# Expert outputs added to rows of the output in memory, a narrower table, 28 rooms, and first weights copied by VectorE alone

## The reference

```python
h = _layernorm(x, axis=-1) * (1 + ca) + sa
x = x + ga * _L0_attn_ref(h, ...)        # 16 heads of 8 features, softmax over 256 tokens
h = _layernorm(x, axis=-1) * (1 + cb) + sb
x = x + gb * _L0_ffn_ref(h, ...)         # 14 experts, each token goes to one
```

## Time and profile before

| | us |
|---|---|
| median of 3 runs | 610.19 (608.88 to 610.45) |
| span of the profiled execution | 609.06 |
| attention loop's last exponential ends | 491.7 |
| first turn that needs a late load (visit 12) | 522.73 |
| last turn (visit 76) | 594.32 |
| last contraction starts | 598.06 |
| last store starts | 601.75 |

### The profile page before, as it was taken

One profiled execution on the slowest core, in us unless ns is written; L12 is line 12 of the kernel. 1 busy time (PEld: TensorE's weight loads), 2 busy tenths in 40 slices (PEclk: granted clock), 3 DMA queues, 4 the chain that ended last, 5 costly groups with the idle time before them and its releaser, 6 DMA issues.

```text
span 609.1 us, 12013 instructions
## 1 busy us (share of the span) xinstructions
PE 471.5 (77%) x2535; PEld 266.9 (44%) x2537; DVE 555.4 (91%) x1419; ACT 545.2 (90%) x2323; POOL 484.3 (80%) x642
## 2 busy tenths in 40 slices
PE   5456887877887777788788788778776688989993
PEld 2113433333343333333334343334333366889992
DVE  5898999999999999999999999999999978788884
ACT  2599999999999999999999999999999963767882
POOL 4566777998999989899998989989898765677763
PEclk9555556566556756655655655675555565999997
DMA  6365544544455555555555555665555215888750
GB/s 194 104 189 157 138 140 125 139 138 140 141 149 148 148 152 140 163 142 167 146 156 149 148 154 148 173 172 145 160 149 152 93 65 143 269 281 255 223 180 27
DMA packets 77072, 94.42 MB, mean 155 GB/s; under 512 B 12806, under 2 KB 60710, under 8 KB 76998
## 3 DMA queue, kind: packets, MB, share of 16 engines
q1 hardware_dynamic: 68842, 75.69, 45.0%
q0 software_dynamic: 6144, 16.82, 7.4%
q10 hardware_dynamic: 2015, 1.15, 0.7%
HBM read 58.41 MB, written 35.20 MB: 154 GB/s over the span
## 4 chain that ended last, share of the span: by engine, by line
ACT 48%; POOL 17%; DVE 12%; PE 11%; issue 8%; DMA 2%; ACTq 1%; POOLq 0%; DVEq 0%; SPq 0%
ACT scores L927 47%; DVE neg_max L1395 4%; PE scores L1223 4%; PE scores L1232 4%; POOL table L838 3%; POOL xhat L787 2%; POOL rstd L770 2%; POOL rest L577 2%; POOL parts L580 2%; POOL h_scaled L810 1%; DVE y_biased_s L1966 1%; DMA table<-rows,place_i 1%; PE scores L1213 1%; POOL xhat L779 1%; POOL att L799 1%
## 5 line engine op out<-in xcount | busy, mean ns | idle before, releaser
L927 ACT ACTIVATE scores<-scores,neg_max 128x256 f32<-128x256 f32 x1024 | 468.5, 827 | 10.5 <-DVE neg_max L1395 10.4
L927 ACT ACTIVATION_READ_ACCUMULATOR scores<-scores,neg_max 128x1 f32 x1024 | 436.2, 588 | 0.0
L1395 DVE TENSOR_REDUCE neg_max<-scores 128x4 f32<-128x1024 f32 x256 | 309.2, 1211 | 7.5 <-PE scores L1073 7.0
L1073 PE MATMUL scores<-k_stack,q_stack 64*128 64x256 bf16 x1024 | 148.5, 389 | 79.3 <-ACT scores L927 67.7
L1073 PEld LDWEIGHTS scores<-k_stack,q_stack 64*128 64x128 bf16 x1024 | 34.0, 106 | 164.3 <-ACT scores L927 120.6
L838 POOL DMA_INDIRECT table<-rows,place_i x64 | 66.0, 1031 | 20.4 <-issue 17.0
L787 POOL TENSOR_SCALAR xhat<-rows,mv,rstd 128x128 f32<-128x128 f32 x60 | 47.6, 796 | 7.1 <-POOL rstd L770 7.1
L893 POOL DMA_INDIRECT out_dram<-x_s x40 | 39.4, 986 | 17.4 <-DVE x_s L1977 9.2
L1232 PE MATMUL scores<-w_s,hid 128*128 x308 | 49.8, 286 | 2.2 <-DVE y_biased_s L1966 1.1
L1101 PE MATMUL side_a<-w_gated,opt_t 128*128 128x128 f32 x128 | 49.7, 491 | 0.0
L779 POOL TENSOR_SCALAR xhat<-x_s,mv,rstd 128x128 f32<-128x128 f32 x62 | 49.1, 801 | 0.4 <-POOL rstd L770 0.4
(11 more groups left out here) (231 smaller groups left out, 876.0 us busy)
## 6 DMA issues: line engine op xcount, KB each, us to landing
q_stack<-parts_dram SPq DMA_DIRECT2D x192, 64.0 KB, 2.9
x_s<-table SPq DMA_DIRECT2D x62, 192.5 KB
parts_dram<-parts SPq DMA_DIRECT2D x31, 384.0 KB, 3.0
k_stack<-parts_dram SPq DMA_DIRECT2D x186, 64.0 KB, 2.2
mod_b<-mod_rows SPq DMA_DIRECT2D x32, 256.0 KB, 4.4
x_s<-in_x_dram SPq DMA_DIRECT2D x13, 256.0 KB, 4.8
table<-pad_tile SPq DMA_DIRECT2D x15, 192.5 KB
more_rooms<-table SPq DMA_DIRECT2D x15, 192.5 KB
```

Of the source, the lines that this page charges most:

```text
L927: last = act.activation(buf[:, k * L:k * L + L], buf[:, k * L:k * L + L], ACT.Exp, bias=neg_max[:, p, n:n + 1], accum_out=exp_sum[:, p, n: ...
L1073: last = pe.matmul(scores[:, c, at:at + L], q_stack[p][r, g + j, t * P:t * P + P], k_stack[p][r, g + j, :], start=True, stop=True)
L1395: dve.tensor_reduce(to, scores[:, (PAIRS * b.n + i) % RING, :].rearrange("p (e j m) -> p e j m", e=2, j=2), AX_X, ALU.max, negate=True).th ...
```

## The change

- **Adding stores.** `store` and `store_packed` get `compute_op=ALU.add`: the indirect DMA adds the rows to what lies in the output. `out_y` goes, and `gate_y` writes in place into the room; it is written one step later, where `out_y` stood.
- **x2 is stored by itself.** `residual` writes x2 into a ring of two tiles. SP stores it to the output as it is, in token order, one plain DMA per batch (`store_x2`), ahead of `store_parts`. `residual` waits for the store of two batches before; GpSimd waits for all of these stores before its first adding ones. The wait for `scattered` moves from `residual` to where h2 is written (`modulate2`, `shift_h2`).
- **Narrow rows.** ROW is 257 words: h2, GW and ID. Scatters, pads and loads shrink by a third.
- **28 rooms.** All lie over x; `more_rooms` goes.
- **First weights.** VectorE copies them for all visits. `by_act`, `fetched` and `fetch_shared` go, with ScalarE's loads of expert numbers.

```diff
-H2, X2, GW, ID = 0, D, 2 * D, 3 * D
-ROW = 3 * D + 1
+H2, GW, ID = 0, D, 2 * D
+ROW = 2 * D + 1
...
-MORE = 5
-ROOMS = SLOTS + MORE
+ROOMS = 28
...
+            def store_x2(b):
+
+                r = b.slot(RING_X2)
+                sp.wait_ge(x2_ready, b.done())
+                sp.dma_start(out_tiles[:, LT * b.n:LT * b.n + LT, :], x2[r][:, :, :]).then_inc(x2_stored[r], 16)
...
+                if b.ago(2).there():
+                    store_x2(b.ago(2))
                 if b.ago(-2).there():
                     store_parts(b.ago(-2))
...
             def modulate2(b):
                 pool.wait_ge(xhat2_ready, b.done())
+                need(pool, scattered[b.slot(RING_ROWS)], 16 * LT * b.earlier(RING_ROWS))
...
+                for r in range(RING_X2):
+                    pool.wait_ge(x2_stored[r], 16 * len(range(r, B - 2, RING_X2)))
                 store(0)
...
-                                        room[:, GW:GW + D], None).then_inc(out_stored[n % SLOTS], 16)
+                                        room[:, GW:GW + D], None, compute_op=ALU.add).then_inc(out_stored[n % SLOTS], 16)
...
-                r = b.slot(RING_ROWS)
-                need(dve, scattered[r], 16 * LT * b.earlier(RING_ROWS))
-                dve.tensor_tensor(rows[r][:, :, X2:X2 + D], x2_p.rearrange("p (t d) -> p t d", t=LT),
+                r = b.slot(RING_X2)
+                need(dve, x2_stored[r], 16 * b.earlier(RING_X2))
+                need(dve, xhat2_ready, b.n - 1)
+                dve.tensor_tensor(x2[r][:, :, :], x2_p.rearrange("p (t d) -> p t d", t=LT),
...
             def gate_y(n):
+                values = rows_in[n % ROOMS][:, GW:GW + D]
                 dve.wait_ge(y_biased, n + 1)
-                dve.tensor_tensor(y_gated_s[:, n % 2, :], y_biased_s[:, n % 2, :], rows_in[n % ROOMS][:, GW:GW + D],
-                                  ALU.mult).then_inc(y_gated, 1)
-
-            def out_y(n):
-                room = rows_in[n % ROOMS]
-                dve.wait_ge(y_gated, n + 1)
-                dve.tensor_tensor(room[:, GW:GW + D], y_gated_s[:, n % 2, :], room[:, X2:X2 + D], ALU.add).then_inc(out_ready, 1)
+                dve.tensor_tensor(values, y_biased_s[:, n % 2, :], values, ALU.mult).then_inc(out_ready, 1)
...
-                if in_range(j + 1) and not by_act(j + 1):
+                if in_range(j + 1):
                     fetch_w1(j + 1)
...
                     if n > PRIMED + 1:
-                        out_y(n - 1)
-                    if in_range(n):
-                        gate_y(n)
+                        gate_y(n - 1)
```

More of the change, by code:

```diff
@@ L78 @@
 W1X = F + FH
+assert ROOMS * ROW + (BUFS_W1 - BUFS) * W1X <= T * D
 X_LATE = 12
@@ L167 @@
 RING_H = 6
+RING_X2 = 2
 def marking(b):
@@ L246, in shared_reload @@
     return min(SLOTS, SHARED - v) if v is not None and v % SLOTS == 0 else 0
-def by_act(q):
-    v = shared_of_visit(q)
-    return v is not None and v % 2 == 1
-def fetched(q):
-    return sum(1 for k in range(q + 1) if not by_act(k)), sum(1 for k in range(q + 1) if by_act(k))
 def merged_by(k):
@@ L310, in build_adaln_attention_moe @@
         out_rows = out.rearrange("b l d -> (b l) d")
+        out_tiles = out.rearrange("b (t p) d -> p (b t) d", p=P)
         ident_s = sb("ident_s", [P, P])
@@ L346, in build_adaln_attention_moe @@
         x_s = sb("x_s", [P, T, D])
-        more_rooms = sb("more_rooms", [P, MORE, ROW])
         q_stack = [sb(f"q_stack{p}", [P, HALF, L], BF16) for p in range(2)]
@@ L370, in build_adaln_attention_moe @@
         rows = [sb(f"rows{r}", [P, LT, ROW]) for r in range(RING_ROWS)]
+        x2 = [sb(f"x2_{r}", [P, LT, D]) for r in range(RING_X2)]
         logit_s = sb("logit_s", [P, 2 * LT, E])
@@ L423, in build_adaln_attention_moe @@
         packed_now = sb("packed_now", [1, 2 * SLOTS], I32)
-        rows_in = [x_room[:, s * ROW:s * ROW + ROW] for s in range(SLOTS)]
-        rows_in += [more_rooms[:, s, :] for s in range(MORE)]
+        rows_in = [x_room[:, s * ROW:s * ROW + ROW] for s in range(ROOMS)]
         x_t = sb("x_t", [P, BUFS, P])
         w1_ring = sb("w1_ring", [P, BUFS, W1X])
-        after_rows = SLOTS * ROW
+        after_rows = ROOMS * ROW
         w1_e = [w1_ring[:, k, :] for k in range(BUFS)]
@@ L432, in build_adaln_attention_moe @@
         y_biased_s = sb("y_biased_s", [P, 2, D])
-        y_gated_s = sb("y_gated_s", [P, 2, D])
         scores = ps("scores", [P, RING, 1024])
@@ L515, in build_adaln_attention_moe @@
         x2_ready = sem("x2_ready")
+        x2_stored = [sem(f"x2_stored{r}") for r in range(RING_X2)]
         xhat2_ready = sem("xhat2_ready")
@@ L543, in build_adaln_attention_moe @@
         w1_ready = sem("w1_ready")
-        w1_copied = sem("w1_copied")
         hid_done = sem("hid_done")
@@ L548, in build_adaln_attention_moe @@
         y_biased = sem("y_biased")
-        y_gated = sem("y_gated")
         out_ready = sem("out_ready")
@@ L703, in fill_ends @@
             def fill_ends():
+                store_x2(Batch(B - 2))
+                store_x2(Batch(B - 1))
                 sp.wait_ge(pad_stored, 16 * len(PADS))
@@ L786, in normalise_x2 @@
                 for t in range(LT):
-                    last = pool.tensor_scalar(xhat2[:, t, :], rows[b.slot(RING_ROWS)][:, t, X2:X2 + D], mv[:, 1, t, 0:1],
+                    last = pool.tensor_scalar(xhat2[:, t, :], x2[b.slot(RING_X2)][:, t, :], mv[:, 1, t, 0:1],
                                               rstd[:, 1, LT + t:LT + t + 1], ALU.subtract, ALU.mult)
@@ L899, in store_packed @@
                 pool.indirect_dma_start(out_rows, bass.IndirectOffsetOnAxis(ap=packed[:, k, D:OUT], axis=0),
-                                        packed[:, k, 0:D].bitcast(F32), None).then_inc(packed_stored, 16)
+                                        packed[:, k, 0:D].bitcast(F32), None, compute_op=ALU.add).then_inc(packed_stored, 16)
             over_batches(iteration, drain)
+            for r in range(RING_X2):
+                pool.wait_ge(x2_stored[r], 16 * len(range(r, B, RING_X2)))
             for n, k in STORES[FIRST:]:
@@ L977, in drain @@
                 act.activation(table_first[:, 4:6], ident_s[:, 0:2], ACT.Gelu)
-            shared_experts = []
-            def fetch_shared(j):
-                v = shared_of_visit(j)
-                need(act, hid_ready, j - BUFS_W1 + 1)
-                act.copy(w1_e[j % BUFS_W1], w1x_s[:, ds(shared_experts[v], 1), :].rearrange("p o f -> p (o f)")).then_inc(w1_copied, 1)
             def tile(j, s, turn):
-                if shared_of_visit(j) == 0:
-                    act.wait_ge(map_ready, 2)
-                if shared_reload(j):
-                    shared_experts.extend(load_many(act, expert_now, SHARED_COL + shared_of_visit(j), shared_reload(j), 0, E - 1))
                 if in_range(j):
@@ L1216, in expand @@
                 pe.wait_ge(x_t_ready, n + 1)
-                from_dve, from_act = fetched(n)
-                pe.wait_ge(w1_ready, from_dve)
-                need(pe, w1_copied, from_act)
+                pe.wait_ge(w1_ready, n + 1)
                 need(pe, hid_ready, n - 1)
@@ L1330, in x2_row @@
             def x2_row(b, t):
-                return rows[b.slot(RING_ROWS)][:, t, X2:X2 + D]
+                return x2[b.slot(RING_X2)][:, t, :]
             def stats_x(b):
@@ L1370, in shift_h2 @@
                 dve.wait_ge(rstd_ready, count)
+                need(dve, scattered[b.slot(RING_ROWS)], 16 * LT * b.earlier(RING_ROWS))
                 steps.after(step["scaled"])
@@ L1965, in bias_y @@
                 dve.wait_ge(y_done, n + 1)
+                need(dve, out_ready, n - 1)
                 dve.tensor_tensor(y_biased_s[:, k, :], expert_out[k],
@@ L1990, in whole_y @@
                 gate_y(n)
-                out_y(n)
             def tile(j, s, turn):
```

2 lines of the change are left out of this document (removed).

## The result

| | before | after |
|---|---|---|
| median, us | 609.54 (6 runs, 607.33 to 610.76) | 637.46 (6 runs, 635.65 to 638.22) |
| span of the profiled execution | 609.06 | 636.3 |
| last exponential starts | 491.27 | 490.85 |
| visit 12 turns | 522.73 | 522.11 |
| visits 22 to 27, from turn to turn | 6.40 | 5.01 |

A visit turns when its transpose starts on TensorE. The last exponential of the kernel before lasts 0.80 us and so ends at 492.07, not at the 491.7 of the table of times before. The changed kernel takes 1.046 times as long, with an interval of 1.0437 to 1.0483. The forecast was 607.6 with a range up to 622.0, so both the sign and the range were wrong.

A forecast was written before the change was run, and what follows sets the result against it. ScalarE's exponentials bound the attention loop, then TensorE the expert stage, held up by register pauses and VectorE, with GpSimd 4.2 us spare. 609.06 - 3.3 + 0.7 = 606.5, 607.6 on the median's scale; range 605.0 to 622.0.

The forecast's parts named there:

- Part 6: Adding stores on GpSimd: 0.7 us more once at the end, and no extra GpSimd time per store.
- x = 0: An adding store's extra GpSimd time over a plain one, taken as 0 within bounds of 0 and 0.96 us.
- Rival A: GpSimd becomes the bound in the expert stage, time 606.6 + 56x us, x being extra time per store; chance 0.31.
- turning point of 0.064 us: Extra GpSimd time per adding store from which the changed kernel would be worse than before.
- The landing, +0.7: At the end, the last adding store lands 0.7 us later than a plain one, bounds 0 and 2.44.
- Part 1: Expert stage and drain: removing VectorE's 77 sums takes 3.3 us off the path.
- Rival B: VectorE's relief stays hidden in the expert stage: 0.8 gained, 0.7 lost, 610.1 us; chance 0.12.
- Part 2: Shared visits: 13 first-weight copies move from ScalarE to VectorE, hidden under TensorE, 0 us; 2.6 without cover.
- Rival C: VectorE's copies lock GpSimd out, 0.29 us in 13 more visits, 3.8 us on GpSimd, 610.4 us; chance 0.03.
- Parts 3 and 4: Expert-stage loads: narrow rows gain 0 us (bounds 0 and 0.5), and 28 rooms gain 0.
- Part 5: Attention loop: x2's 32 plain stores on SP sit in a 2.9 us hole, 0 us; 12 us without it.
- Rival D: The attention loop suffers from x2's stores, 608.8 to 619.6 us, put at 614; chance 0.04.

The follow-up runs named there:

- experiment 3: The changed kernel with adding stores only for the 13 packed tiles and plain ones for whole visits: 613.64 us, ratio 1.0067.
- experiment 5: The changed kernel with its whole-visit stores in six forms, adding or plain, of 128, 64 or 16 rows: 627.41 us in a single execution.
- experiment 1: The changed kernel with plain stores instead of adding ones, leaving x2 out of the output: 604.03 us, ratio 0.9925.
- kernels 7 to 10: The kernel before with ScalarE copying first weights for seven more whole visits, once for all odd 15 to 49, once with a shorter drain: 608.05 to 609.51 us.
- experiment 2: The kernel before with only the addition put into both indirect stores: 638.37 us, ratio 1.0473.
- experiment 6: The changed kernel with plain stores, x2 left out, and ScalarE copying first weights for 13 shared visits as before: 606.76 us, ratio 0.9953.
- experiment 4: The changed kernel with 21 rooms instead of 28: 636.51 us, ratio 1.0447.
- kernel 8: The kernel before with ScalarE copying first weights also for odd whole visits 15 to 49, with a second load of expert numbers: 609.51 us, ratio 0.9992.
- kernels 7 and 10: One program run twice, the kernel before with ScalarE copying first weights also for seven whole visits: 609.02 us (ratio 0.9981) and 608.29 us (0.9976).

## Why the prediction was wrong, point by point

**Part 6, the step that failed: x = 0.** The store of 512-byte rows and the scatter of 1540-byte rows, 0.962 and 0.963 us, show that bytes don't count. They say nothing of another operation in the DMA, and the text said so and still took the lower bound. Measured is x = 0.585, within the bounds of 0 and 0.96. **Rival A** then holds, in mechanism and size: it puts the last store's start at 597.5 + 56 x 0.585 = 630.3 us, measured 629.76, and the time at 606.6 + 32.8 = 639.4; the profiled execution took 638.15 and the median is 637.46. Its turning point of 0.064 us fits, though no run lies near it: with 13 adding stores, 7.8 us in all in place of 56x, the sum gives 614.4, and experiment 3 measured 613.64. The fixed half microsecond of experiment 5 is the term that stood at nothing. The upper end of the range, 622.0, came from cutting A at x = 0.27, although its bound of 0.96 stood in the text.

**The landing, +0.7.** The tile view's median of 3.3 us has the plain stores of x2 in it. The stores of whole visits alone have, from issue to landing, in the changed kernel:

```profile
DMA to landing us min/median/max: 3.2/3.6/7.0
```

and plain ones in experiment 1:

```profile
DMA to landing us min/median/max: 2.5/2.5/4.6
```

Medians say little here: in kernels 7 to 10, with plain stores, they are 3.4 to 4.2 us. The shortest landings say more: 3.2 us in all three kernels whose stores all add, 2.2 to 2.9 in the kernels with plain ones, and 0.6 of the difference is the longer instruction. So hardly anything beyond the instruction is seen, and at the end nothing. From the last store's start to the end of the span it is 7.3 us before (601.75 to 609.06) and in experiment 1, and 7.9 in experiment 3, as much more as the instruction is longer. In the changed kernel and in experiment 2 it is 6.5 and 6.6. There SP's wait for TensorE at the closing barrier is shorter, 3.0 us against 4.8 before; why is open.

**Part 1, the relief of VectorE, 3.3 us.** Right in direction, and in size as far as the runs tell. Experiments 1 and 6 take 4.9 and 2.7 us off the median, on both sides of 3.3. But no run takes away the sum alone: both have the narrow rows, the rooms and x2's own stores too. Single traces, against that of before, in us:

| | forecast | 1 | 6 |
|---|---|---|---|
| visit 12 turns | 0.3 | 2.69 | 0.62 |
| visit 12 to 76 | 2.0 | 3.51 | 3.33 |
| visit 76 to the span's end | 1.0 | 0.66 | 0.51 |

Visits 22 to 27 take 5.17 and 5.19 us, so this term is 1.2 as forecast, and visits 32 to 34 give 0.47 for the 0.4. What the sum missed are 0.45 us in visits 12 to 22, 0.46 us between the turns of 27 and 28, and small pieces in later visits. The end was sized too large, at 1.0. In the drain, experiment 6 with a clock like that of before gives 0.62: two sums stand there ahead of the last routing, that of visit 1 (506.46) as well as that of visit 0, and the prediction counted one, which would fit. The other 2 us of experiment 1 go with the clock. The prediction took the clock as 1.00 in the windows that matter; in the drain it was 0.53 and 0.50 in the same trace, and that is where executions of one kernel part. Rival B falls: the turns of visits 22 to 27 are at the 5.2 us that confirm the first term.

**Part 2, the copies, 0.** Right by the traces, 68.26 against 68.08 us between visits 12 and 76; the times alone don't settle it. **Rival C** falls: in experiment 6, with 13 copies fewer on VectorE, the packed stores have 957/962/1058 ns, in experiment 1 957/959/1070, so none is longer by a copy's 0.29. The Trainium skill, "SBUF — State Buffer", section "SBUF: two separate sides", gives such a copy as a lock against DMAs issued from GpSimd; the 0.962 and 0.959 us don't show it.

**Parts 3 and 4, narrow rows and 28 rooms, 0.** Rooms: right by experiment 4. Narrow rows were not run alone. The scatters keep their length. The 0.46 us between the turns of 27 and 28 don't need them: kernel 8, with wide rows, has 1.88 us there, experiment 1 1.91, before 2.37.

**Part 5, x2's stores on SP, 0.** Right: the attention loop does not end later. In the changed kernel the store sits in the hole of the earlier trace rows: it starts at 309.19, parts at 313.39.

```profile
309.19 0.58 SPq L649 DMA_DIRECT2D out_dram<-x  x1
313.39 0.38 SPq L600 DMA_DIRECT2D parts_dram<-parts  x1
```

Its issue is 0.58 us instead of the assumed 0.38, which changes nothing. **Rival D** falls: the last exponential starts at 490.85.

## What to carry to other kernels

A DMA that also computes is a different instruction for the engine that issues it: price it by a row of its own kind, and where there is none, let the range reach to the bound, above all where a nearly full queue multiplies the price. Ask first how much spare time the issuing engine has: here 0.064 us per store was all that the forecast's sum allowed, and all the rest of the change was worth 2.7 to 4.9 us against 29 (experiment 2 against before) to 33 us (the changed kernel against experiment 1) for 64 dearer stores. In this kernel, whose store queue was full either way, seven more buffers ahead of it gained nothing. And before a difference of 1 or 2 us between two traces is put down to an edit, look at the granted clock beside it and, if it can be had, at a second trace of the same program: here two of them differed by 2.8 us at one place.

## What the runs showed of the hardware

- An adding indirect DMA costs GpSimd 1.547 us for 128 rows, a plain one 0.96; the difference is 0.52 us at 16 rows, 0.51 at 64 and 0.61 at 128, so mostly fixed. A plain one is mostly fixed too: 0.866, 0.930 and 0.989 us.
- It moves 112 packets more for 128 rows. The landings of the changed kernel's adding stores of whole visits took 3.2 to 7.0 us with a median of 3.6, the plain ones of experiment 1 2.5 to 4.6 with 2.5; the medians of plain ones reach 4.2 in other kernels.
- In the drain, from 505 to 510 us, TensorE's granted clock was 0.50 to 0.54 in some profiled executions and 0.66 to 1.00 in others with nearly the same work. In kernels 7 and 10, the same program, it was 0.51 and 0.94, and visit 12 turned at 522.82 and 520.00.
